# Earlier aggregation loads, other chunk counts in batch 0, and an x conversion moved ahead of a batch's last root

## The chip, the cores and the metric

The kernel runs on one core of a Trainium2 chip. The metric is the device time of one launch in microseconds; 1651.48 us is the median of three runs before the change.

## The reference

Eight batches of x (2048 rows of 512), one adjacency matrix (2048 x 2048, 0 or 1, about 0.8% ones), weights W (512 x 1024) and a bias.

```python
Wi, Wj = (W[:, :Din], W[:, Din:])
mi = jnp.einsum('bkd,od->bko', x, Wi)
mj = jnp.einsum('bkd,od->bko', x, Wj)
a = adj.astype(x.dtype)
deg = a.sum(axis=1)
out = deg[None, :, None] * (mi + b) + jnp.einsum('ij,bjo->bio', a, mj)
...
x = _layernorm(x + out, axis=-1)
```

## The kernel before

A batch is 16 tiles of 128 rows. Each batch has two phases. In the **projection** PE computes mj (half h = 0) and mi (h = 1) for each tile. fp32 products are made of fp32r matmuls: `parts` (ScalarE, lines 430 and 432) turns a tile of x into `x_hi` and `x_lo`, `difference` (POOL, line 268) makes `x_df`, and `project` (PE) runs 4 cross matmuls (line 330) and 8 main ones (lines 338 and 340) per half, 24 per tile. ScalarE copies the cross result out of PSUM (`take_cross`), VectorE combines (lines 559 and 566) and splits the next x (`split_x`, lines 548 and 551), ScalarE takes mj_hi (line 445) and POOL mj_lo (line 273). mi goes to DRAM (`store_mi`, line 179) and comes back later (`load_mi`, line 198). Tiles 0 and 1 of batch 0 are computed natively (`project_native`, line 315) from `x_first` and the weights as loaded (`w_stage`), while VectorE splits the weights (`split_w`, lines 527 to 533, last part `W_df`).

In the **aggregation** PE multiplies the adjacency matrix with mj, 32 matmuls (line 362) per tile into one of two PSUM buffers. ScalarE widens the adjacency columns of tile i+2 to fp32r when tile i is done (`widen`, line 457). POOL adds the bias to the reloaded mi (`add_bias`, line 279), VectorE forms `residual` (line 594: deg * mi + x in a ring of four buffers r) and then `normalise` (lines 600 to 619), for which ScalarE gives the square root (`root`, line 461). SyncE stores the tile (line 246). Aggregation tile i may start when VectorE has summed tile i-2 (line 600).

The adjacency matrix arrives during batch 0 as 64 chunks through four buffers (`load_chunk`, line 175): ScalarE casts each to int8 (`cast_chunk`, line 452), VectorE adds it into the degree sums (`count_chunk`, lines 577 and 580), and a chunk load waits for both of the chunk four before it. Every 16 chunks PE sums them over partitions (`degrees`, line 347) and VectorE takes the result (`take_degrees`, line 585). The lists say how many chunks are handled in each tile:

```python
PROJ_CHUNKS = [0, 0, 2, 2, 2, 2, 2, 2, 2, 2, 2, 2, 2, 2, 2, 2]
AGG_CHUNKS = [4, 3, 3, 3, 3, 4, 4, 4, 4, 4, 0, 0, 0, 0, 0, 0]
```

Each engine's order is written out by hand and the engines meet only at semaphores. SyncE issues all loads and stores but those of x_raw, which ScalarE issues. At the end of a batch's projection SyncE issues five loads for the aggregation (mi of tiles 0 and 1, x of tiles 0, 1, 2 into r). In VectorE's order residual(0) stands behind the projection, then for each tile come its counts, residual(i+1) and normalise(i). Batch 0 is unrolled; batches 1 to 6 are one hardware loop, batch 7 a copy, with inner hardware loops over groups of four tiles.

Of the kernel before, what the change touches and what calls it, by code (L numbers as in the profile page):

```python
# [5 lines left out]
def bass_adj_resnorm(nc, x, xt, adjt, wt, b, out):  # L6
# [33 lines left out]
    with ctx:  # L40
# [90 lines left out]
        norm_ready = sem("norm_ready")  # L131
        out_stored = [sem(f"out_stored{s}") for s in range(GT)]
# [5 lines left out]
        AGG_CHUNKS = [4, 3, 3, 3, 3, 4, 4, 4, 4, 4, 0, 0, 0, 0, 0, 0]  # L138
# [31 lines left out]
        def _(sp):  # L170
# [11 lines left out]
            for c in range(DK, 2 * DK):  # L182
                sp.dma_start(w_stage[c][:, :], wt[c]).then_inc(w_loaded[c], 16)
# [19 lines left out]
            def batch(bt):  # L203
                zero = known(bt) and bt == 0
                base = NT * bt

                def proj(g):
                    for u in range(GT):
                        if zero and GT * g + u < NATIVE:
                            continue  # L210
                        if zero:
                            for c in proj_chunks(GT * g + u):
                                load_chunk(c + AB)
                        store_mi(base + GT * g + u)

                over_groups(sp, zero, False, proj)

                sp.wait_ge(mi_stored, 16 * (base + 2))
                for u in range(2):
                    load_mi(base + u, u)  # L220
                for u in range(GT - 1):
                    if not zero:
                        sp.wait_ge(out_stored[u], 16 * NG * bt)
                    load_r(base + u, u)

                def agg(g):
                    for u in range(GT):
# [18 lines left out]
                        sp.dma_start(out_tiles[m], r[u][:, :]).then_inc(out_stored[u], 16)  # L246
# [59 lines left out]
        def _(pe):  # L306
# [60 lines left out]
            def batch(bt):  # L367
# [15 lines left out]
                if zero:  # L383
                    for i in range(NT):
                        if i == 2:
                            degrees(1)
# [22 lines left out]
        def _(act):  # L409
# [52 lines left out]

            for order in range(DK):
# [11 lines left out]
            def batch(bt):  # L475
# [3 lines left out]
                def proj(g):  # L479
                    last_group = known(g) and g == NG - 1  # L480
                    for u in range(GT):
# [4 lines left out]
                        if not (final and last_group and u == GT - 1):  # L486
# [14 lines left out]
                over_groups(act, zero, True, proj)  # L501
                if zero:
                    for i in range(NT):
                        for c in agg_chunks(i):
                            cast_chunk(c)
                        if i < NT - 2:
                            act.wait_ge(agg_done, i + 1)
                            widen(i + 2, i % 2, NT * ((i + 2) // TPB + 1))
                        root(i)
                else:  # L510
# [6 lines left out]
                    for i in range(2):  # L517
                        root(NT * bt + NT - 2 + i)

            over_batches(act, batch)  # L520

        @block.vector
        def _(dve):
# [73 lines left out]
            def normalise(m, u, s):  # L597
# [21 lines left out]
                nc.vector.tensor_scalar(r[u][:, :], r[u][:, :], mean_var[:, 0:1], inv_std[:, :],  # L619
                                        ALU.subtract, ALU.mult).then_inc(norm_ready, 1)  # L620
# [11 lines left out]
            def batch(bt):  # L632
# [25 lines left out]
                def agg(g):  # L658
                    for u in range(GT):
                        i = GT * g + u  # L660
                        m = base + i
                        if zero:
                            for c in agg_chunks(i):
                                count_chunk(c)
                            if i == 2:
# [8 lines left out]
                        normalise(m, u, u % 2)  # L674
# [41 lines left out]
```

## Time and profile before

| what | us |
|---|---|
| median of three runs | 1651.48 (1648.02 to 1652.07) |
| the profiled execution | 1650.52 |
| its span | 1648.7 |
| PE busy (matmul) | 1637.6 |
| VectorE busy | 848.3 |
| ScalarE busy | 662.3 |
| POOL busy | 499.8 |

The mean granted TensorE clock of the span is 0.998 of full speed. The span is from the first to the last instruction; the profiled execution's time holds 1.8 us beside it. Busy time says which engine is never long idle; the rest is read from the starts of PE's matmuls and from what ended each engine's idle time.

### The profile page before, as it was taken

The numbers are of one execution on the slowest core, as the hardware profiler recorded it, in microseconds if no ns is written. First come the engines' busy times: TensorE is split into PE (matmuls) and PEld (weight loads), VectorE is DVE, ScalarE is ACT, GpSimd is POOL, SyncE is SP. The second block draws the span as 40 slices with busy tenths as digits, with TensorE's granted clock in tenths as the row PEclk, the third lists the DMA queues.
The fourth block names the chain that finished last, engine by engine and source line by source line (L and its number), as shares of the span: only waits on it lengthen the run. The fifth ranks groups of instructions, "written<-read, shape, count | busy, mean of one in ns | idle before, by whom it ended". The sixth has DMA issues, their size and how long they took to land.

```text
span 1648.7 us, 24789 instructions
## 1 busy us (share of the span) xinstructions
PE 1637.6 (99%) x7196; PEld 1347.3 (82%) x7196; DVE 848.3 (51%) x1878; ACT 662.3 (40%) x964; POOL 499.8 (30%) x386
## 2 busy tenths in 40 slices
PE   9999999999999999999999999999999999999998
PEld 6878888888888888888888888888888888888886
DVE  8778644445445444445444445445444445444544
ACT  5755434423353324533245322453325522255221
POOL 3531134311343113431144311442114421154210
PEclk9999999999999999999999999999999999999999
DMA  6667423333223332343322432233323243232332
GB/s 198 196 197 240 147 77 102 128 108 96 89 90 127 115 95 83 99 131 102 95 95 89 134 109 87 90 102 126 109 83 101 90 138 104 76 102 83 128 115 70
DMA packets 102698, 187.26 MB, mean 114 GB/s; under 512 B 11408, under 2 KB 11408, under 8 KB 102672
## 3 DMA queue, kind: packets, MB, share of 16 engines
q1 hardware_dynamic: 84816, 154.44, 29.4%
q10 hardware_dynamic: 17856, 32.51, 6.4%
q8 instruction: 11, 0.18, 0.0%
q14 instruction: 15, 0.12, 0.0%
HBM read 119.80 MB, written 67.11 MB: 113 GB/s over the span
## 4 chain that ended last, share of the span: by engine, by line
PE 91%; issue 2%; DVE 1%; DMA 0%; POOL 0%; DVEq 0%; SPq 0%; ACT 0%; POOLq 0%
PE agg_ps L362 54%; PE cross_ps L330 12%; PE main_ps L340 12%; PE main_ps L338 12%; DMA mi_in<-mi_dram 0%; POOL mi_in L279 0%; DVE deg_part L580 0%; DVEq L601 0%; DVE r L600 0%; DVE stats L602 0%; POOL x_df L268 0%; DVE r L619 0%; PE deg_ps L347 0%; DVE newton L611 0%; SPq L246 0%
## 5 line engine op out<-in xcount | busy, mean ns | idle before, releaser
L362 PE MATMUL agg_ps<-mj_hi,adjT 128*128 128x512 f32 x2048 | 798.0, 390 | 1.7 <-DVE r L600 1.7
L362 PE MATMUL agg_ps<-mj_lo,adjT 128*128 128x512 f32 x2048 | 797.5, 389 | 0.0
L457 ACT ACTIVATE adjT<-adjT 128x2048 fp32r (+1 forms) x128 | 245.2, 1916 | 532.4 <-PE agg_ps L362 532.4
L362 PEld LDWEIGHTS agg_ps<-mj_hi,adjT 128*128 128x128 f32 x2048 | 385.0, 188 | 81.7 <-DVE r L600 1.8
L362 PEld LDWEIGHTS agg_ps<-mj_lo,adjT 128*128 128x128 f32 x2048 | 385.0, 188 | 80.0
L338 PE MATMUL main_ps<-W_hi,x_hi 128*128 128x512 f32 x1008 | 392.3, 389 | 0.0
L340 PE MATMUL main_ps<-W_lo,x_lo 128*128 128x512 f32 x1008 | 392.2, 389 | 0.0
L279 POOL TENSOR_TENSOR mi_in<-mi_in,bias 128x512 f32<-128x512 f32 x128 | 166.1, 1300 | 655.9 <-DMA mi_in<-mi_dram 655.8
L330 PE MATMUL cross_ps<-W_df,x_df 128*128 128x512 f32 x1008 | 270.8, 390 | 1.0 <-DVE W_df L533 0.5
L273 POOL TENSOR_TENSOR mj_lo<-mj,mj_hi 128x512 f32 (+1 forms) x126 | 169.7, 1347 | 269.7 <-ACT mj_hi L445 269.7
L600 DVE TENSOR_TENSOR r<-agg_ps,r 128x512 f32<-128x512 f32 x128 | 88.4, 691 | 315.7 <-PE agg_ps L362 315.7
L441 ACT ACTIVATE cross<-cross_ps 128x512 f32<-128x512 f32 x252 | 148.4, 589 | 209.7 <-PE cross_ps L330 208.2
L268 POOL TENSOR_TENSOR x_df<-x_top,x_lo 128x512 fp32r<-128x512 f32 x126 | 163.9, 1301 | 202.9 <-ACT x_lo L432 202.7
L330 PEld LDWEIGHTS cross_ps<-W_df,x_df 128*128 128x128 f32 x1008 | 188.4, 188 | 43.3 <-ACT cross L441 2.7
L338 PEld LDWEIGHTS main_ps<-W_hi,x_hi 128*128 128x128 f32 x1008 | 189.2, 188 | 39.7 <-DVE mi L566 0.2
L340 PEld LDWEIGHTS main_ps<-W_lo,x_lo 128*128 128x128 f32 x1008 | 189.2, 188 | 39.4
L559 DVE SCALAR_TENSOR_TENSOR mj<-main_ps,cross 128x512 f32<-128x512 f32 x126 | 87.0, 690 | 215.1 <-PE main_ps L340 208.4
L566 DVE SCALAR_TENSOR_TENSOR mi<-main_ps,cross 128x512 f32<-128x512 f32 x126 | 87.0, 691 | 115.9 <-PE main_ps L340 102.3
L594 DVE SCALAR_TENSOR_TENSOR r<-mi_in,deg,r 128x512 f32<-128x512 f32 x128 | 98.0, 768 | 53.6 <-DMA r<-in_x 42.3
L430 ACT ACTIVATE x_hi<-x_top 128x512 fp32r<-128x512 f32 x126 | 79.6, 632 | 66.1 <-PE main_ps L340 63.0
L602 DVE BATCH_NORM_STATS2 stats<-r 128x6 f32<-128x512 f32 x128 | 88.9, 695 | 11.7
L551 DVE TENSOR_TENSOR x_raw<-x_raw,x_top 128x512 f32<-128x512 f32 x126 | 87.2, 692 | 4.3
(59 smaller groups left out, 600.3 us busy)
## 6 DMA issues: line engine op xcount, KB each, us to landing
mi_dram<-mi SPq DMA_DIRECT2D x128, 256.0 KB, 2.1
mi_in<-mi_dram SPq DMA_DIRECT2D x128, 256.0 KB, 2.7
r<-in_x SPq DMA_DIRECT2D x128, 256.0 KB, 2.7
out<-r SPq DMA_DIRECT2D x128, 256.0 KB, 2.1
x_raw<-in_xt ACTq DMA_DIRECT2D x124, 256.0 KB, 2.8
adj_in<-in_adjt SPq DMA_DIRECT2D x64, 256.0 KB, 3.6
r<-in_wt SPq DMA_DIRECT2D x4, 256.0 KB, 5.4
adj_in<-in_xt SPq DMA_DIRECT2D x2, 256.0 KB, 3.8
```

The lines of the kernel that those rows point to most:

```text
L268: pool.tensor_tensor(x_df[s][:, :], x_top[:, :], x_lo[s][:, :].bitcast(fp32), ALU.subtract).then_inc(x_df_ready, 1)
L273: pool.tensor_tensor(mj_lo[:, bass.ds(t, 1), :].rearrange("p t d -> p (t d)"), mj[:, :], mj_hi[:, bass.ds(t, 1), :].rearrange("p t d -> p ...
L279: pool.tensor_tensor(mi_in[u % 2][:, :], mi_in[u % 2][:, :], bias[:, :], ALU.add).then_inc(mib_ready, 1)
L330: last = nc.tensor.matmul(cross_ps[h][:, :], x_df[s][:, k * P:(k + 1) * P], W_df[:, half * DK + k, :], start=(k == 0), stop=(k == DK - 1))
L338: nc.tensor.matmul(main_ps[h][:, :], x_hi[s][:, k * P:(k + 1) * P], W_hi[:, half * DK + k, :], start=(k == 0), stop=False)
L340: last = nc.tensor.matmul(main_ps[h][:, :], x_lo[s][:, k * P:(k + 1) * P], W_lo[:, half * DK + k, :], start=False, stop=(k == DK - 1))
L362: last = nc.tensor.matmul(agg_ps[s][:, :], adjT[s][:, j, :], part[:, j, :], start=(j == 0 and part is mj_hi), stop=(j == NT - 1 and part i ...
L441: nc.scalar.activation(cross[h][:, :], cross_ps[h][:, :], ACT.Copy).then_inc(cross_ready, 1)
L457: nc.scalar.activation(adjT[s][:, :, :], adjT8[:, :, bass.ds(i * P, P)], ACT.Copy).then_inc(adjT_ready, 1)
L594: nc.vector.scalar_tensor_tensor(r[u][:, :], mi_in[u % 2][:, :], deg[:, bass.ds(i, 1)], r[u][:, :], ALU.mult, ALU.add).then_inc(res_ready, 1)
L600: nc.vector.tensor_tensor(r[u][:, :], agg_ps[s][:, :], r[u][:, :], ALU.add).then_inc(sum_ready, 1)
L602: nc.vector.bn_stats(stats[:, :], r[u][:, :]).then_inc(ln_step, 1)
```

## The change

Five edits. (1) `first_loads` (the five loads) is issued by SyncE in the last projection group behind the store of its second tile (tile 13), in every batch; in batch 0 the store of mi also goes ahead of a tile's last chunk load. (2) In batch 0 the chunk counts per aggregation tile are other ones, and the degree step of chunks 16 to 31 stands ahead of tile 3 instead of 2. (3) ScalarE converts x of the next batch's tile 1 ahead of the root of a batch's last tile, and not in the next batch's first tile; its group loop is therefore split. (4) The first weight block is loaded from ScalarE's queue. (5) The last tile of the last batch is scaled in two halves of the columns, and the second half is stored by ScalarE.

```diff
@@ -129,13 +129,14 @@
         ln_step = sem("ln_step")
         std_ready = sem("std_ready")
         norm_ready = sem("norm_ready")
+        last_stored = sem("last_stored")
         out_stored = [sem(f"out_stored{s}") for s in range(GT)]
 
         block = ctx.enter_context(nc.Block())
 
         CHUNKS = IB * NT
         PROJ_CHUNKS = [0, 0, 2, 2, 2, 2, 2, 2, 2, 2, 2, 2, 2, 2, 2, 2]
-        AGG_CHUNKS = [4, 3, 3, 3, 3, 4, 4, 4, 4, 4, 0, 0, 0, 0, 0, 0]
+        AGG_CHUNKS = [2, 3, 3, 3, 3, 3, 3, 4, 4, 4, 4, 0, 0, 0, 0, 0]
 
         def proj_chunks(t):
             first = sum(PROJ_CHUNKS[:t])
@@ -179,7 +180,7 @@
                 sp.dma_start(mi_dram[n], mi[:, :]).then_inc(mi_stored, 16)
 
             sp.dma_start(x_first[0], xt[0]).then_inc(x_first_loaded[0], 16)
-            for c in range(DK, 2 * DK):
+            for c in range(DK + 1, 2 * DK):
                 sp.dma_start(w_stage[c][:, :], wt[c]).then_inc(w_loaded[c], 16)
             sp.dma_start(x_first[1], xt[1]).then_inc(x_first_loaded[1], 16)
             for c in range(DK):
@@ -202,26 +203,35 @@
 
             def batch(bt):
                 zero = known(bt) and bt == 0
+                final = known(bt) and bt == NB - 1
                 base = NT * bt
+
+                def first_loads():
+                    if zero:
+                        sp.wait_ge(w_ready, 2 * DK)
+                        sp.wait_ge(main_done, 2 * NATIVE)
+                    sp.wait_ge(mi_stored, 16 * (base + 2))
+                    for u in range(2):
+                        load_mi(base + u, u)
+                    for u in range(GT - 1):
+                        if not zero:
+                            sp.wait_ge(out_stored[u], 16 * NG * bt)
+                        load_r(base + u, u)
 
                 def proj(g):
                     for u in range(GT):
                         if zero and GT * g + u < NATIVE:
                             continue
                         if zero:
-                            for c in proj_chunks(GT * g + u):
+                            for c in proj_chunks(GT * g + u)[:-1]:
                                 load_chunk(c + AB)
                         store_mi(base + GT * g + u)
-
-                over_groups(sp, zero, False, proj)
-
-                sp.wait_ge(mi_stored, 16 * (base + 2))
-                for u in range(2):
-                    load_mi(base + u, u)
-                for u in range(GT - 1):
-                    if not zero:
-                        sp.wait_ge(out_stored[u], 16 * NG * bt)
-                    load_r(base + u, u)
+                        if zero:
+                            load_chunk(proj_chunks(GT * g + u)[-1] + AB)
+                        if known(g) and g == NG - 1 and u == 1:
+                            first_loads()
+
+                over_groups(sp, zero, True, proj)
 
                 def agg(g):
                     for u in range(GT):
@@ -243,7 +253,10 @@
                                 if c + AB < CHUNKS:
                                     load_chunk(c + AB)
                         sp.wait_ge(norm_ready, m + 1)
-                        sp.dma_start(out_tiles[m], r[u][:, :]).then_inc(out_stored[u], 16)
+                        if final and ending and u == GT - 1:
+                            sp.dma_start(out_tiles[m, :, 0:DO // 2], r[u][:, 0:DO // 2]).then_inc(out_stored[u], 16)
+                        else:
+                            sp.dma_start(out_tiles[m], r[u][:, :]).then_inc(out_stored[u], 16)
 
                 agg(0)
                 if zero:
@@ -382,7 +395,7 @@
 
                 if zero:
                     for i in range(NT):
-                        if i == 2:
+                        if i == 3:
                             degrees(1)
                         if i == 7:
                             degrees(2)
@@ -460,6 +473,7 @@
                 act.wait_ge(ln_step, LN * m + 3)
                 nc.scalar.activation(std[:, :], var_eps[:, :], ACT.Sqrt).then_inc(std_ready, 1)
 
+            act.dma_start(w_stage[DK][:, :], wt[DK]).then_inc(w_loaded[DK], 16)
             for order in range(DK):
                 copy_w_hi(DK + order, order)
             native_mj_hi(0)
@@ -483,7 +497,7 @@
                         n = NT * bt + t
                         if zero and t < NATIVE:
                             continue
-                        if not (final and last_group and u == GT - 1):
+                        if not (final and last_group and u == GT - 1) and (zero or not (known(g) and t == 0)):
                             parts(n + 1, (u + 1) % 2)
                         take_cross(n, 0)
                         if not (final and last_group and u >= GT - 3):
@@ -498,7 +512,14 @@
                         if last_group and u in (0, 2):
                             widen(u // 2, u // 2, NT if zero else None)
 
-                over_groups(act, zero, True, proj)
+                if zero:
+                    for g in range(NG):
+                        proj(g)
+                else:
+                    proj(0)
+                    with act.Fori(1, NG - 1) as g:
+                        proj(g)
+                    proj(NG - 1)
                 if zero:
                     for i in range(NT):
                         for c in agg_chunks(i):
@@ -506,6 +527,8 @@
                         if i < NT - 2:
                             act.wait_ge(agg_done, i + 1)
                             widen(i + 2, i % 2, NT * ((i + 2) // TPB + 1))
+                        if i == NT - 1:
+                            parts(NT + 1, 1)
                         root(i)
                 else:
                     with act.Fori(0, NP - 1) as k:
@@ -515,9 +538,14 @@
                             widen(2 * k + i + 2, i, None)
                             root(m)
                     for i in range(2):
+                        if i == 1 and not final:
+                            parts(NT * bt + NT + 1, 1)
                         root(NT * bt + NT - 2 + i)
 
             over_batches(act, batch)
+            act.wait_ge(norm_ready, TILES + 1)
+            act.dma_start(out_tiles[TILES - 1, :, DO // 2:DO], r[GT - 1][:, DO // 2:DO]).then_inc(last_stored, 16)
+            act.wait_ge(last_stored, 16)
 
         @block.vector
         def _(dve):
@@ -594,7 +622,7 @@
                 nc.vector.scalar_tensor_tensor(r[u][:, :], mi_in[u % 2][:, :], deg[:, bass.ds(i, 1)], r[u][:, :],
                                                ALU.mult, ALU.add).then_inc(res_ready, 1)
 
-            def normalise(m, u, s):
+            def normalise(m, u, s, last_tile):
                 dve.wait_ge(res_ready, m + 1)
                 dve.wait_ge(agg_done, m + 1)
                 nc.vector.tensor_tensor(r[u][:, :], agg_ps[s][:, :], r[u][:, :], ALU.add).then_inc(sum_ready, 1)
@@ -616,8 +644,9 @@
                 dve.wait_ge(ln_step, LN * m + 6)
                 nc.vector.tensor_tensor(inv_std[:, :], inv0[:, :], newton[:, 1:2], ALU.mult).then_inc(ln_step, 1)
                 dve.wait_ge(ln_step, LN * m + 7)
-                nc.vector.tensor_scalar(r[u][:, :], r[u][:, :], mean_var[:, 0:1], inv_std[:, :],
-                                        ALU.subtract, ALU.mult).then_inc(norm_ready, 1)
+                for cols in ((slice(0, DO // 2), slice(DO // 2, DO)) if last_tile else (slice(0, DO),)):
+                    nc.vector.tensor_scalar(r[u][:, cols], r[u][:, cols], mean_var[:, 0:1], inv_std[:, :],
+                                            ALU.subtract, ALU.mult).then_inc(norm_ready, 1)
 
             for order in range(DK):
                 split_w(DK + order, order)
@@ -662,7 +691,7 @@
                         if zero:
                             for c in agg_chunks(i):
                                 count_chunk(c)
-                            if i == 2:
+                            if i == 3:
                                 take_degrees(1)
                             if i == 7:
                                 take_degrees(2)
@@ -671,7 +700,7 @@
                         ending = known(g) and g == NG - 1 and u == GT - 1
                         if not ending:
                             residual(m + 1, i + 1, (u + 1) % GT, 16 * (NG * bt + g + 1 + (u + 1) // GT))
-                        normalise(m, u, u % 2)
+                        normalise(m, u, u % 2, final and ending)
 
                 if zero:
                     for g in range(NG):
```

## Rows read from the trace of the kernel before

**Rows 1.** The page, busy time: engine, us, share, instructions.

```profile
PE 1637.6 (99%) x7196; PEld 1347.3 (82%) x7196; DVE 848.3 (51%) x1878; ACT 662.3 (40%) x964; POOL 499.8 (30%) x386
```

**Rows 2.** Timeline of PE, 110 to 118: start, us, engine, line, operation, idle before.

```profile
110.87 0.39 PE L362 MATMUL agg_ps<-mj_lo,adjT 128*128 128x512 f32 x1
112.19 0.61 PE L347 MATMUL deg_ps<-ones,deg_part 128*128 128x2 f32 x4 [0.94 <-DVE deg_part L580]
114.47 0.79 PE L362 MATMUL agg_ps<-mj_hi,adjT 128*128 128x512 f32 x1 [1.67 <-DVE r L600]
115.06 0.63 PE L362 MATMUL agg_ps<-mj_lo,adjT 128*128 128x512 f32 x1
...
117.92 0.40 PE L362 MATMUL agg_ps<-mj_hi,adjT 128*128 128x512 f32 x1
```

**Rows 3.** Timeline of PE around a later degree step.

```profile
152.38 0.50 PE L347 MATMUL deg_ps<-ones,deg_part 128*128 128x2 f32 x4
...
153.07 0.40 PE L362 MATMUL agg_ps<-mj_lo,adjT 128*128 128x512 f32 x1
```

**Rows 4.** Timeline of the other engines, 89 to 109.

```profile
89.69 0.42 SPq L179 DMA_DIRECT2D mi_dram<-mi  x1
...
92.75 2.05 SPq L175 DMA_DIRECT2D adj_in<-in_adjt  x2
...
96.17 1.82 POOL L273 TENSOR_TENSOR mj_lo<-mj,mj_hi 128x512 fp32r<-128x512 f32 x1 [0.62 <-ACT mj_hi L445]
...
101.40 0.96 SPq L198 DMA_DIRECT2D mi_in<-mi_dram  x2
...
105.93 2.67 POOL L279 TENSOR_TENSOR mi_in<-mi_in,bias 128x512 f32<-128x512 f32 x2 [7.94 <-DMA mi_in<-mi_dram]
105.97 1.28 ACT L461 ACT_TABLE_LOAD   x1
107.98 1.17 DVE L594 SCALAR_TENSOR_TENSOR r<-mi_in,deg,r 128x512 f32<-128x512 f32 x1 [7.51 <-POOL mi_in L279]
```

**Rows 5.** Timeline of PE and POOL at two passages between batches.

```profile
426.28 1.29 POOL L268 TENSOR_TENSOR x_df<-x_top,x_lo 128x512 fp32r<-128x512 f32 x1 [17.70 <-ACT x_lo L432]
...
427.02 0.39 PE L340 MATMUL main_ps<-W_lo,x_lo 128*128 128x512 f32 x1
427.70 0.72 PE L330 MATMUL cross_ps<-W_df,x_df 128*128 128x512 f32 x2 [0.30 <-POOL x_df L268]
...
429.97 1.29 POOL L268 TENSOR_TENSOR x_df<-x_top,x_lo 128x512 fp32r<-128x512 f32 x1
...
630.71 0.39 PE L340 MATMUL main_ps<-W_lo,x_lo 128*128 128x512 f32 x1
631.14 0.72 PE L330 MATMUL cross_ps<-W_df,x_df 128*128 128x512 f32 x2
```

**Rows 6.** Timeline of VectorE in later aggregation tiles of batch 0, and in the last tile.

```profile
158.39 2.28 DVE L580 TENSOR_TENSOR deg_part<-deg_part,adj_in 128x512 fp32r<-128x512 f32 x3 [0.54 <-DMA adj_in<-in_adjt]
...
168.71 0.68 DVE L600 TENSOR_TENSOR r<-agg_ps,r 128x512 f32<-128x512 f32 x1
...
172.21 3.07 DVE L580 TENSOR_TENSOR deg_part<-deg_part,adj_in 128x512 fp32r<-128x512 f32 x4
...
1642.60 0.69 DVE L600 TENSOR_TENSOR r<-agg_ps,r 128x512 f32<-128x512 f32 x1 [3.66 <-PE agg_ps L362]
```

**Rows 7.** Timeline of the start: SyncE, VectorE, PE.

```profile
1.19 0.90 SPq L183 DMA_DIRECT2D mi_in<-in_wt  x2
...
4.33 0.43 DVE L527 TENSOR_SCALAR adjT<-mi_in 128x512 uint32<-128x512 uint32 x1 [4.33 <-DMA mi_in<-in_wt]
...
22.00 1.20 PE L330 MATMUL cross_ps<-W_df,x_df 128*128 128x512 f32 x4 [0.47 <-DVE W_df L533]
```

**Rows 8.** Timeline of the end.

```profile
1645.64 0.55 DVE L619 TENSOR_SCALAR r<-r,mean_var,inv_std 128x512 f32<-128x512 f32 x1
1646.22 0.33 SPq L246 DMA_DIRECT2D out<-r  x1
```

## The prediction

> **What bounds the kernel now.** I read the page first: PE is busy for 1637.6 of 1648.7 us [rows 1]. So no engine's speed is at issue; only the stretches in which PE's matmuls do not follow each other at their full beat can be won. I then went along PE's timeline and took the distances between the starts of matmuls. A matmul normally starts 0.227 us after the one before it (1637.6 us over 7196 matmuls gives 0.228; 32 of them make an aggregation tile, 7.26 us; 24 make a projection tile, 5.44 us). Four kinds of places break the beat.
>
> First, one stall in batch 0 ahead of aggregation tile 2 [rows 2]. After the matmul at 110.87 the small degree matmuls come at 112.19, tile 2 starts only at 114.47, and then matmuls start 0.43 us apart (115.06 - 114.47 is even 0.59): the clock has gone to 1.2 GHz, its lower level, after PE had run two matmul groups with waits of 1 to 2 us. By 117.92 the beat is full again (2.4 GHz). Second, five of the seven passages from one batch to the next lose a little at the start of projection tile 1 [rows 5]. Third, PE waits at 22.00 for the weights' third part [rows 7]. Fourth, after the last matmul some 6 us of normalising and storing follow, in which PE does nothing [rows 8].
>
> **Part 1, the stall in batch 0.** From 110.87 to 117.92 are 7.05 us. The work in it is nine full-beat matmuls, 9 x 0.227 = 2.04 us, and the degree step. What a degree step costs where nobody waits is seen ahead of tile 7 [rows 3]: 153.07 - 152.38 = 0.69, less one beat = 0.46 us. So 7.05 - 2.04 - 0.46 = 4.55 us are lost, the slow clock included.
>
> The cause, followed back [rows 4]: PE's tile 2 needs VectorE's sum of tile 0 (line 600), which is queued behind residual(0), four counts and residual(1). residual(0) started only at 107.98, after 7.51 us of waiting for POOL's bias, which waited 7.94 us for the load of mi that SyncE issued at 101.40, behind all projection stores and chunk loads. The degree matmuls moreover waited for chunk 31, the fourth of those counts.
>
> The change puts the five loads behind the store of tile 13, which was issued at 89.69 to 90.11. Five issues take what they took before, 0.96 us for the two of mi (101.40) and about 1.45 for the three of r, so they end near 92.55; SyncE had its next issue at 92.75 anyway, waiting for a count. The queue's order costs nothing there. The two stores that now follow five transfers could land later: the mi load needed 4.5 us from issue (101.40) to POOL's start at 105.93 in traffic, so I put the last of five at 97 to 98, and the store of tile 14 at about 98 to 100. VectorE's copy of tile 15 waits for that store; nobody on PE waits for this copy until the next batch. POOL becomes free at 96.17 + 1.82 = 97.99 and adds the bias by 99.3 and 100.6. VectorE then does residual(0) around 100.5 to 102.5, two counts instead of four (2 x 0.77, as four take 3.07 at 172.21 [rows 6]), residual(1) 0.75, so it is ready for the sum of tile 0 between 103 and 106, while PE ends tile 0 only at 103.85. The sum ends by 107 at the latest, and PE asks for it at 111.1: cover of at least 4 us. One thing becomes late next, without reaching PE: the square root's table load (1.28 us at 105.97) now stands in tile 0's normalisation and delays it about 1 us; tile 1's sum then comes near 112.0 and is asked for at 118.8. I take the full 4.55 us. Bounds: 4.6 above; below, 1.6 if the stall shrinks only until the clock holds (the eight matmuls from 114.47 to 117.92 took 3.45 instead of 1.81).
>
> **The moved counts.** Chunks per tile go from 4,3,3,3,3,4,4,4,4,4 to 2,3,3,3,3,3,3,4,4,4,4. The total is 36 both times, so no work is saved; what moves is who has slack. The degree step of tile 3 needs chunk 31, counted in tile 1: a tile of slack. That of tile 7 needs chunk 47, now counted during tile 6, and that of tile 11 needs chunk 63, now counted during tile 10; both had a whole tile of slack before. Working for the latter [rows 6]: the sum starts at 168.71 and the four counts of the next tile end at 172.21 + 3.07 = 175.28, 6.57 us later. A sum that waits for PE starts about 0.26 us after the end of its tile (1642.60, where the last matmul starts at 1642.11 and is due for 0.23), so the last count ends 6.83 us into a tile of 7.26: 0.43 us of slack. For tile 7, with three counts, it is 1.2 us. VectorE also waited 0.54 us for a chunk at 158.39. One such wait exceeds the slack of tile 11 by 0.1. I take 0, and 0 to 0.8 us of loss as range.
>
> **Part 2, the batch passages.** The last matmul of tile 0 starts at 427.02, tile 1 at 427.70 [rows 5]: 0.45 us over the beat, and 0.15 more until the beat is regained, 0.60 together. At 630.71 to 631.14 it is 0.20 + 0.13 = 0.33; three further passages (834, 1038, 1241) show the same 0.33. Passages 218.8 and 1444 show 0.03. Tile 1 waited for x_df, which POOL computed at 426.28 after ScalarE's two conversions, which stand behind the square root of the last tile. The change issues both conversions ahead of that root. Their inputs were split at the end of the projection, so they run while ScalarE would wait for tile 15; 1.2 us of ScalarE and 1.3 of POOL hidden under a 7.26 us tile. What is late next is the copy of cross 0, which used to come after the two conversions and comes 1.1 us earlier without them, well ahead of PE. Gain: 0.60 + 4 x 0.33 less 5 x 0.03 = 1.8 us (bounds 1.2 and 1.9).
>
> **Part 3, the start.** SyncE issues x first and the first weight at 1.19; VectorE starts on it at 4.33 and its chain of splits ends in the wait at 22.00 [rows 7]. ScalarE can issue that load beside SyncE's, 0.44 us earlier. The transfers share their engines, so I take 0.3 us for VectorE's chain. PE's own first matmul is bound by the 28 warm-up matmuls, but at 22.00 (idle 0.47, 0.64 off the beat) and at the tile after it PE waits on VectorE's chain, more than 0.3 in sum, so the 0.3 arrives. Bounds: 0 and 0.44. If ScalarE's table load (1.28 long) came ahead of the issue, the weight would be 0.85 late instead.
>
> **Part 4, the end.** The last scaling takes 0.55 us at 1645.64, the store is issued at 1646.22 [rows 8]. In two halves the first store goes out about 0.2 us sooner, the second about 0.1 later from another queue, each with half the bytes. I take 0.25 us, bounds -0.3 and +0.5 (no half-size store is in the trace).
>
> **Other edits.** The store ahead of the second chunk load, and the unrolled loops of SyncE and ScalarE, cost nothing where those engines wait for others. In ScalarE's new loop the parts of tile 2 follow a loop entry; x_df of tile 2 ended at 429.97 + 1.29 = 431.26 and PE asked for it at about 433.3, 2.0 us of cover.
>
> **Sum**: 4.55 + 1.8 + 0.3 + 0.25 = 6.9 us. The profiled execution took 1650.52 us (span 1648.7), the median of three is 1651.48, 0.96 above it. Against its own time the sum gives 1643.6; the comparison is with the median, so I forecast 1651.48 - 6.9 = 1644.6 us.
>
> **Rivals.** (A) Tile 11's degree step waits for chunk 63. For it: 0.43 us of slack against a wait of 0.54 seen once. Against it: the other chunk groups came in time. PE loses 0.3 to 0.8 us, the clock should hold as it did over the 0.45 us gap at 427: about 1645.1, chance 0.14. (B) The two loads or stores on a second queue bring nothing, because the transfers fill the same DMA engines: start and end give 0, 6.35 us remain, 1645.1, chance 0.12. The Trainium skill, "DMA: Bandwidth & Descriptors", section "Issuing engines are not separate DMA queues", says that issuing from several engines saves only the sequencer's issue time; that is this rival, and by it the start could give at most the 0.44 of one issue. (C) The first weight comes late, behind the table load or on a slow first use of the queue: 0.85 us later, and the clock's rise after the warm-up may suffer, 1 to 2 us lost in place of 0.3 won: 1646.4, chance 0.05. (D) The stall stays because something else holds residual(0), such as the crowd of transfers around 90 to 100: then only parts 2 to 4 count, 1649.1, chance 0.07. (E) Slower: entering ScalarE's new loop stops its sequencer (fetching the code) in each of seven batches. It decides from 2.0 us of entry on, the cover of x_df for tile 2; to eat 6.9 us it must be 3.0 us, and 3.7 us for a loss of 0.3%, 1656.4. Nothing near that is in the trace. Chance 0.03.
>
> **Chances.** The forecast has 0.59. A measurement can tell about 0.3% (4.95 us), a time below 1646.5. Forecast, A and B lie below it, but runs of the kernel before scatter by 4 us, so a part of them falls short: faster 0.77, same 0.20 (D, half of C, scatter), slower 0.03. Range: best bounds sum to 7.5 us, with about 2 us for scatter 1642.0; at the top A and C with scatter, 1648.2; D and E stay outside, about 0.1.
>
> **What would show it.** Right: PE's starts stay 0.227 apart through 111 to 118 with the clock at full; residual(0) near 101; tile 1 of each batch on the beat and POOL's x_df for it inside the last aggregation tile; a first split near 4.0. Wrong: a PE wait for deg_part (A), a first split later than 4.33 (C), VectorE waiting for mi_in past 104 (D), PE waiting for x_df of tile 2 (E).

## The result and the profile after

The changed kernel takes 1643.48 us (median of six runs, 1643.4 to 1643.72). Beside it the kernel before took 1651.86 us (1648.02 to 1652.68). The ratio is 0.9952 with a 95% interval of 0.9941 to 0.9962: faster by 0.5%, inside the forecast range, 1.1 us below the forecast 1644.6. The profiled execution took 1643.72 us with a span of 1641.9 (before: 1650.52 and 1648.7).

The changed kernel's page, busy time by engine and the chain of work that ended last by engine:

```profile
PE 1634.2 (100%) x7196; PEld 1346.8 (82%) x7196; DVE 844.8 (51%) x1879; ACT 661.7 (40%) x964; POOL 498.4 (30%) x386
...
PE 98%; DVE 1%; DMA 0%; issue 0%; POOL 0%; ACT 0%; DVEq 0%
```

PE is 3.4 us less busy with the same 7196 matmuls [rows 1]. In the 7.05 us of the old stall it counted as busy for 4.44, where the same matmuls at full beat take 2.5: at the low clock a matmul counts as longer. Most of the rest lies at the passages, where the profile's modelled end of a matmul (0.39 us after its start) covers most of PE's delay. Next, all waits of PE in the changed kernel (engine, line, releaser: us, times, longest):

```profile
PE agg_ps L415 <- POOL ones L277: 1.1, 1, 1.1
PE cross_ps L343 <- DVE W_df L561: 0.5, 1, 0.5
```

The waits for VectorE's sum and for the degree count [rows 2] are gone. Both that remain are in the first 22 us. Around the place of the old stall the timelines of SyncE, POOL, VectorE and ScalarE read (start, us, engine, line, operation, idle before):

```profile
88.00 0.34 SPq L180 DMA_DIRECT2D mi_dram<-mi  x1
...
89.59 0.92 SPq L199 DMA_DIRECT2D mi_in<-mi_dram  x2
...
90.56 1.38 SPq L202 DMA_DIRECT2D r<-in_x  x3
...
92.58 0.33 SPq L176 DMA_DIRECT2D adj_in<-in_adjt  x1
...
97.66 2.99 POOL L292 TENSOR_TENSOR mi_in<-mi_in,bias 128x512 f32<-128x512 f32 x2
...
101.12 0.74 DVE L622 SCALAR_TENSOR_TENSOR r<-mi_in,deg,r 128x512 f32<-128x512 f32 x1
...
101.79 1.48 DVE L608 TENSOR_TENSOR deg_part<-deg_part,adj_in 128x512 fp32r<-128x512 f32 x2
...
103.18 0.75 DVE L622 SCALAR_TENSOR_TENSOR r<-mi_in,deg,r 128x512 f32<-128x512 f32 x1
...
103.98 0.69 DVE L628 TENSOR_TENSOR r<-agg_ps,r 128x512 f32<-128x512 f32 x1
...
105.84 1.28 ACT L474 ACT_TABLE_LOAD   x1
```

Against [rows 4]: SyncE issues the loads at 89.59 instead of 101.40, POOL adds the bias at 97.66 instead of 105.93, residual(0) starts at 101.12 instead of 107.98, and tile 0's sum at 103.98, as soon as PE has finished that tile. PE asks for it at 111.0, so some 6 us of cover stand here. The five issues fit ahead of SyncE's next one at 92.58.

PE itself runs through, and the granted clock stays up. PE's timeline from tile 1 to tile 2:

```profile
110.74 0.39 PE L375 MATMUL agg_ps<-mj_lo,adjT 128*128 128x512 f32 x1
110.96 0.39 PE L375 MATMUL agg_ps<-mj_hi,adjT 128*128 128x512 f32 x1
111.19 0.39 PE L375 MATMUL agg_ps<-mj_lo,adjT 128*128 128x512 f32 x1
```

The stretch of the old stall in the changed kernel (window, its length, busy times of PE, PEld, VectorE, ScalarE and POOL, then granted clock, DMA share, GB/s):

```profile
110.87:117.92 7.05, 7.05 (x33) 5.84 (x32) 5.90 (x14) 3.90 (x5) 1.30 (x1) 1.00 0.75 253
```

At the first passage inside the batch loop, POOL's x_df for tile 1 now lies in the last aggregation tile, 9 us before PE needs it, and PE keeps its beat (422.34 to 422.56), against 0.68 us at 427.02 [rows 5]:

```profile
413.44 1.44 POOL L281 TENSOR_TENSOR x_df<-x_top,x_lo 128x512 fp32r<-128x512 f32 x1 [9.66 <-ACT x_lo L445]
...
422.34 0.39 PE L353 MATMUL main_ps<-W_lo,x_lo 128*128 128x512 f32 x1
422.56 0.62 PE L343 MATMUL cross_ps<-W_df,x_df 128*128 128x512 f32 x2
```

**Where the time went, by the two traces.** The matmuls are the same in number and order, so the start of one and the same matmul can be compared. Just ahead of the old stall it is 110.87 before and 110.74 after: 0.13 us won at the start, less than the scatter there (see the experiments). The first matmul of aggregation tile 7 of batch 0 starts at 152.74 and 148.10: 4.64, so 4.51 at the stall. The last matmul starts at 1642.11 and 1635.45: 6.65 (from unrounded starts), so 2.0 at the passages. From the last matmul to the end of the span it is 6.59 and 6.45: 0.14 at the end. In sum 6.8 us. The medians differ by more, 8.4, and the kernel before scatters by over 4 us where the new one stays within 0.3. Half of the study is about that difference.

### The profile page after: what moved, and what is told of

Read it like the earlier page. It is cut to its first block, busy times and chain, and to the rows that moved or that the text cites. A ratio compares the mean times of both kernels' runs of the same rounds, so it can differ in the third digit from the quotient of the medians.

```text
span 1641.9 us, 24654 instructions
## 1 busy us (share of the span) xinstructions
PE 1634.2 (100%) x7196; PEld 1346.8 (82%) x7196; DVE 844.8 (51%) x1879; ACT 661.7 (40%) x964; POOL 498.4 (30%) x386
## 4 chain that ended last, share of the span: by engine, by line
PE 98%; DVE 1%; DMA 0%; issue 0%; POOL 0%; ACT 0%; DVEq 0%
PE agg_ps L375 57%; PE cross_ps L343 14%; PE main_ps L351 14%; PE main_ps L353 14%; DVE W_lo L558 0%; DVE W_df L561 0%; DMA mi_in<-in_wt 0%; DVE adjT L555 0%; DVE x_raw L579 0%; DVE mj_lo L568 0%; PE deg_ps L360 0%; POOL x_df L281 0%; DVE x_top L576 0%; DVE stats L630 0%; DVE r L628 0%
## 5 line engine op out<-in xcount | busy, mean ns | idle before, releaser
L622 DVE SCALAR_TENSOR_TENSOR r<-mi_in,deg,r 128x512 f32<-128x512 f32 x128 | 101.4, 796 | 13.1 <-POOL mi_in L292 9.2
```

Source lines behind the costliest of these rows:

```text
L622: nc.vector.scalar_tensor_tensor(r[u][:, :], mi_in[u % 2][:, :], deg[:, bass.ds(i, 1)], r[u][:, :], ALU.mult, ALU.add).then_inc(res_ready, 1)
```

## The experiments

Each kernel below is an edit of the changed kernel, except one. Beside each group of them the kernel before ran along; its medians were 1649.4, 1650.4 and 1651.1 us. With the six runs beside the result that makes 65 runs from 1647.71 to 1654.84, median 1650.72, so the change is worth 7.1 us against all of them and the 8.4 holds part of this scatter. The new kernel's median hardly moves, so I compare with it.

**The base again.** No edit.

> The changed kernel once more, as the base for the others: 1643.5 us, its runs within 0.3 us of each other. If the small scatter of its first six runs was luck, it spreads over 2 to 4 us like the kernel before.

Measured: 1643.65 us, 1643.59 to 1643.80 over five runs; ratio to before 0.9965 [0.9951, 0.9978]. The kernel before, in eleven runs beside it: 1647.89 to 1651.36. The small scatter belongs to the new kernel.

**One edit taken back at a time, small ones.**

```diff
u1_weight_on_sync
-            for c in range(DK + 1, 2 * DK):
+            for c in range(DK, 2 * DK):
...
-            act.dma_start(w_stage[DK][:, :], wt[DK]).then_inc(w_loaded[DK], 16)
```

> The changed kernel with the first weight block loaded from SyncE's queue again. My theory: the gain of this edit is bounded by the shared transfer engines, and the traces of before and after differ by 0.13 us at this place, so 1643.6, 0.1 to 0.2 above the base, first split of VectorE at 4.3. The rival, that the issue time of 0.44 us arrives in full as I forecast in part: 1643.8 or more.

Measured: 1643.70 us (1643.62 to 1644.08), 0.05 above the base. The first split of the changed kernel starts at 4.15 instead of 4.33, although the load is issued 0.44 earlier:

```profile
0.75 0.42 ACTq L476 DMA_DIRECT2D mi_in<-in_wt  x1
0.75 0.39 SPq L182 DMA_DIRECT2D adj_in<-in_xt  x1
...
4.15 0.43 DVE L555 TENSOR_SCALAR adjT<-mi_in 128x512 uint32<-128x512 uint32 x1 [4.15 <-DMA mi_in<-in_wt]
```

Against the kernel before 0.18 of 0.44 us reached VectorE; against u1's own trace, where the first split starts at 4.25, it is 0.10. The median shows 0.05. What reached PE stays open: the last matmul ahead of the old stall starts at 110.87, 111.05 and 111.12 in the three traces with the load on SyncE's queue behind x (the kernel before, u1, w2 below), and anywhere from 110.49 to 111.73 in those with it on ScalarE's.

```diff
u2_whole_last_store
-                        if final and ending and u == GT - 1:
-                            sp.dma_start(out_tiles[m, :, 0:DO // 2], r[u][:, 0:DO // 2]).then_inc(out_stored[u], 16)
-                        else:
-                            sp.dma_start(out_tiles[m], r[u][:, :]).then_inc(out_stored[u], 16)
+                        sp.dma_start(out_tiles[m], r[u][:, :]).then_inc(out_stored[u], 16)
...
-                        normalise(m, u, u % 2, final and ending)
+                        normalise(m, u, u % 2, False)
```

> The changed kernel with the last tile scaled and stored whole. By the traces of before and after the end shrank by 0.15 us, so 1643.65. Rival: the halves gain nothing and the 0.15 was scatter of one transfer, 1643.5.

Measured: 1643.87 us (1643.61 to 1643.88), 0.22 above the base. With one run at the base's level this is small but goes the expected way. The traces are clearer: from the last matmul to the end it is 6.59 to 6.60 us in the three with a whole last store, and 6.45 to 6.49 in all others.

**The passages.**

```diff
u3_conversion_late
-                        if not (final and last_group and u == GT - 1) and (zero or not (known(g) and t == 0)):
+                        if not (final and last_group and u == GT - 1):
                             parts(n + 1, (u + 1) % 2)
...
-                        if i == NT - 1:
-                            parts(NT + 1, 1)
...
-                        if i == 1 and not final:
-                            parts(NT * bt + NT + 1, 1)
```

> The changed kernel with the x conversion of a batch's tile 1 back behind the last root. My theory: five passages lose 0.33 to 0.60 again, 2.0 us in sum, 1645.5, and PE waits for x_df at the start of tile 1 there. Rival: the passages' loss came from ScalarE's loop entries and not from the conversion; then it stays at 1643.5, since the loop stays split here.

Measured: 1644.60 us (1644.28 to 1644.85), 0.95 above the base. Both expectations missed: a late conversion costs half of what the traces had shown. What was left in u3 was ScalarE's split loop, so the next kernel put the one loop back too.

```diff
w1_conversion_late_one_loop (beside the edit of u3)
-                if zero:
-                    for g in range(NG):
-                        proj(g)
-                else:
-                    proj(0)
-                    with act.Fori(1, NG - 1) as g:
-                        proj(g)
-                    proj(NG - 1)
+                over_groups(act, zero, True, proj)
```

> As u3_conversion_late, and ScalarE's groups again in one loop as in the kernel before. u3 cost 1.0 us and not the 2.0 that the traces of before and after differ by. Theory: the other 1.0 is the loop entry that stood ahead of the conversion at each passage and is gone with the unrolled first group; then this kernel is at 1645.6 and its five passages lose 0.60 and 4 x 0.33 in the trace. Rival: the rest was scatter or came from elsewhere (the early loads), 1644.6.

Measured: 1645.96 us (1645.66 to 1646.49), 2.3 above the base. The two traces side by side, u3 first: ScalarE's root and conversion at the first looped passage and PE at the next one.

```profile
419.79 0.20 ACT L474 ACTIVATE std<-var_eps 128x1 f32<-128x1 f32 x1 [7.35 <-DVE var_eps L630]
420.31 0.63 ACT L443 ACTIVATE x_hi<-x_top 128x512 fp32r<-128x512 f32 x1 [0.32 <-PE main_ps L353]
...
625.99 0.39 PE L353 MATMUL main_ps<-W_lo,x_lo 128*128 128x512 f32 x1
626.22 0.73 PE L343 MATMUL cross_ps<-W_df,x_df 128*128 128x512 f32 x2
```

```profile
419.64 0.20 ACT L474 ACTIVATE std<-var_eps 128x1 f32<-128x1 f32 x1 [7.34 <-DVE var_eps L623]
420.37 0.63 ACT L443 ACTIVATE x_hi<-x_top 128x512 fp32r<-128x512 f32 x1 [0.52 <-PE main_ps L353]
...
626.04 0.39 PE L353 MATMUL main_ps<-W_lo,x_lo 128*128 128x512 f32 x1
626.47 0.49 PE L343 MATMUL cross_ps<-W_df,x_df 128*128 128x512 f32 x1
```

From the root to the conversion ScalarE takes 0.52 us without a loop entry between them and 0.73 with one. These 0.2 us arrive in full at PE: from the last matmul of tile 0 to the first of tile 1 it is 0.23 us in u3 and 0.43 in w1, the old gap. From the last matmul of batch 0 to the last of all PE takes 1421.65 us in the changed kernel, 1422.62 in u3, 1423.64 in w1 and 1423.66 in the kernel before. So with the conversion late, root and conversion cost 0.97 us and the loop entry another 1.02, five times 0.2. A kernel with the conversion early and one loop was not run: the early conversion may take away both, since the entry then stands behind it.

**The stall: which part carries it.**

```diff
u4_loads_late
-                        if known(g) and g == NG - 1 and u == 1:
-                            first_loads()

                 over_groups(sp, zero, True, proj)
+                first_loads()
```

> The changed kernel with the five loads issued behind the whole projection again; the new chunk counts stay. Theory 1 (the stall was one queue on VectorE, and either part removes most of it): residual(0) near 108, then two counts, residual(1), and the sum of tile 0 ends near 112.1 instead of 114.4; PE waits 0.4 to 1.9 us ahead of tile 2, too short for the clock to fall: 1644.0 to 1645.4, runs close together. Theory 2 (the early loads carry the whole gain, the counts nothing): PE waits as before and the clock falls, about 1648.

Measured: 1644.59 us (eight runs 1644.02 to 1645.16, one 1648.22), 0.9 above the base. Theory 1 holds in size, but not in detail. The one run at 1648.22 has a mean granted clock of 0.998 where the others have 0.999 or more, so "too short for the clock to fall" does not hold for all. And in its trace, of the fastest run, PE's tile 2 is late by a tenth of a microsecond only, because stores ahead of chunk loads let the five loads out at 99.71 rather than 101.40, and VectorE has two counts less. So the changed store order has a share in u4's small loss, and where the median's 0.9 us lie this trace does not show:

```profile
106.33 1.75 DVE L621 SCALAR_TENSOR_TENSOR r<-mi_in,deg,r 128x512 f32<-128x512 f32 x1 [7.13 <-POOL mi_in L291]
...
110.49 0.39 PE L374 MATMUL agg_ps<-mj_lo,adjT 128*128 128x512 f32 x1
110.80 0.50 PE L374 MATMUL agg_ps<-mj_hi,adjT 128*128 128x512 f32 x1
```

```diff
u5_old_counts
-        AGG_CHUNKS = [2, 3, 3, 3, 3, 3, 3, 4, 4, 4, 4, 0, 0, 0, 0, 0]
+        AGG_CHUNKS = [4, 3, 3, 3, 3, 4, 4, 4, 4, 4, 0, 0, 0, 0, 0, 0]
...
-                        if i == 3:
+                        if i == 2:
                             degrees(1)
...
-                            if i == 3:
+                            if i == 2:
                                 take_degrees(1)
```

> The changed kernel with the chunk counts 4,3,3,3,3,4,4,4,4,4 and the degree step ahead of tile 2 again; the loads stay early. Theory 1: residual(0) at 101, four counts end by about 105.5 and the sum by 107, before PE asks at 111: no wait, 1643.5. Theory 3 (the loads alone are not enough, since four counts and the degree step hold tile 2): PE waits 1 us or more, 1644.5 to 1648.

Measured: 1643.60 us (1643.40 to 1643.64), the base's time. With early loads the counts change nothing, as theory 1 has it.

u6_both_back has the edits of u4 and u5 together.

> The changed kernel with both parts of the stall back (late loads, old counts); start, passages and end stay as changed. Theory 1: the stall is whole again, +4.5 us or more by the trace. Theory 4 (the scatter of the kernel before, 1648.0 to 1652.7, comes from how long the clock stays at its low level behind this stall): the runs spread over 2 us or more, between about 1646 and 1650. If the scatter had another source they stay within 0.5 us of each other near 1648.

Measured: 1647.23 us, 3.6 above the base, eleven runs from 1644.75 to 1649.43. The slowest is the profiled one; its trace loses 5.3 us at the stall. Neither part alone is missed by more than 0.9, both together cost 3.6: they remove the same wait, and their gains do not add. The scatter is back with the stall. The three stretches behind the stall in u6's profiled execution (window, its length, busy times, granted clock, DMA share, GB/s), and below them two of the kernel before:

```profile
114.14:117.50 3.36, 3.36 (x8) 2.68 (x9) 2.69 (x10) 2.13 (x5) 0.00 (x0) 0.50 0.28 104
117.50:120.50 3.00, 3.00 (x8) 2.32 (x8) 2.81 (x5) 1.43 (x1) 0.25 (x1) 0.53 0.61 195
120.60:123.00 2.40, 2.40 (x12) 1.99 (x11) 1.86 (x9) 1.26 (x3) 0.93 (x1) 1.00 0.95 299
```

```profile
114.47:117.80 3.33, 3.33 (x8) 2.65 (x9) 2.65 (x10) 2.10 (x5) 0.00 (x0) 0.51 0.27 100
117.90:121.00 3.10, 3.10 (x15) 2.56 (x14) 2.90 (x5) 1.37 (x1) 0.09 (x1) 1.00 0.63 201
```

PE stayed at 1.2 GHz for over 6 us in u6 and for 3.4 in the kernel before, although the break ahead of it was the shorter one in u6: 3.0 us from the last matmul of tile 1 to the first of tile 2, against 3.6. At that level a matmul starts 0.427 us after the last, 0.2 later than at 2.4 GHz, so u6's stretch costs about 3 us and the other 1.6.

**The gap by itself.** The changed kernel with one wait of PE ahead of tile 2, for a later (v2) or much later (v3) step of tile 1's normalisation.

```diff
+                        if i == 2:
+                            pe.wait_ge(ln_step, LN + 3)      (v2_forced_wait)
+                            pe.wait_ge(norm_ready, 2)        (v3_forced_wait_long)
                         aggregate(0, i, i % 2, i == 0, i >= 2)
```

> The changed kernel with one wait added: PE's aggregation tile 2 of batch 0 waits for the variance of tile 1 (ready near 113.2), so PE idles once for 2.1 us at the place of the old stall and nothing else is late. If only the idle time costs: 1645.8 with runs within 0.4. Theory 4 (the clock falls after such a gap in some runs and for unequal times): 1646 to 1649, spread over 1 us or more, matmuls 0.43 us apart behind the gap.

> As v2_forced_wait, but tile 2 waits for tile 1's scaled result (near 114.9): one idle gap of 3.8 us. If only the idle time costs: 1647.5. Theory 4: the clock falls in nearly every run, so 1.5 to 3.5 us more, 1649 to 1651.

Measured: v2 has two groups. Five runs took 1646.02 to 1646.60 with a mean granted clock of 0.999, six took 1647.77 to 1648.84 with 0.998. Its profiled execution (1646.18) is of the first kind, PE idle for 2.10 us and on the beat at once. The first group is the base plus the gap, 1643.65 + 2.26 = 1645.9; the second adds 1.7 to 2.8 us. That the clock fell in the second group is read from its mean and the time; none of the six was profiled. v3 took 1648.81 to 1650.86 in eleven runs (median 1649.58), none near 1647.5: the gap's 3.9 us and 2 us on top, of which the eight matmuls at the low clock in its trace explain 1.6. (The profiled execution, 1650.40, also came to tile 1's end 1.0 us late, from the start and from a wait shown below.) In v3's trace the clock falls only after PE has resumed:

```profile
115.87 0.50 PE L375 MATMUL agg_ps<-mj_hi,adjT 128*128 128x512 f32 x1 [3.76 <-DVE r L650]
...
116.91 0.51 PE L375 MATMUL agg_ps<-mj_hi,adjT 128*128 128x512 f32 x1
117.22 0.63 PE L375 MATMUL agg_ps<-mj_lo,adjT 128*128 128x512 f32 x1
117.64 0.63 PE L375 MATMUL agg_ps<-mj_hi,adjT 128*128 128x512 f32 x1
```

**The early loads on the kernel before.** Only the five loads move; counts, store order, conversion, start and end are those of before.

```diff
w2_before_early_loads (against the kernel before)
+                def first_loads():
...
                         store_mi(base + GT * g + u)
+                        if known(g) and g == NG - 1 and u == 1:
+                            first_loads()

-                over_groups(sp, zero, False, proj)
-
-                sp.wait_ge(mi_stored, 16 * (base + 2))
-                for u in range(2):
-                    load_mi(base + u, u)
...
+                over_groups(sp, zero, True, proj)
```

> The kernel before with one thing changed: the five loads go out behind the store of tile 13. Theory 1: the stall is gone by this alone, no PE wait between 108 and 118, about 1643.5 + 2.0 (passages) + 0.2 (start and end) = 1645.7. Theory 4 (the scatter belongs to the stall): the runs lie within 0.5 us of each other. If the scatter belongs to something else of the kernel before (the batch passages, the start), they spread over 2 us or more, as before's own do.

Measured: 1647.05 us, 4.0 below the kernel before beside it (1651.09; ratio 0.9976 [0.9967, 0.9985]), so this one move carries about half of the change. But the runs spread from 1646.23 to 1649.73 and the median is 1.3 above what I expected: theory 4 is not the whole story. There is no stall at 111 in its trace. There is one at 61, in the projection, where ScalarE and PE wait for VectorE:

```profile
61.01 0.69 DVE L572 SCALAR_TENSOR_TENSOR mi<-main_ps,cross 128x512 f32<-128x512 f32 x1 [1.75 <-DMA mi_dram<-mi]
...
61.79 0.60 ACT L447 ACTIVATE cross<-cross_ps 128x512 f32<-128x512 f32 x1 [1.48 <-DVE mi L572]
...
61.75 0.19 PEld L344 LDWEIGHTS main_ps<-W_hi,x_hi 128*128 128x128 f32 x1 [0.55 <-DVE mi L572]
61.75 0.50 PE L344 MATMUL main_ps<-W_hi,x_hi 128*128 128x512 f32 x1
```

VectorE may not write mi again before the last mi is stored. The store sat behind chunk loads in SyncE's queue until 56.32, 1.0 us after mi was ready, and landed 4.7 us later; PE waited for VectorE and lost 0.3 us. The waits of that kind in all of a trace, the kernel before first, then w2, then the changed kernel:

```profile
DVE mi L566 <- DMA mi_dram<-mi: 13.2, 12, 2.5
```

```profile
DVE mi L572 <- DMA mi_dram<-mi: 10.8, 11, 2.0
```

```profile
DVE mi L594 <- DMA mi_dram<-mi: 1.8, 2, 1.0
```

In the twelve traces with the store ahead of a tile's last chunk load it occurs one to three times, 0.5 to 2.6 us in sum. But the chain to PE is no mark of the old order: it is there in u1, u6 and v3 too, near 34, and costs most in v3, 0.6 us:

```profile
34.40 0.69 DVE L596 SCALAR_TENSOR_TENSOR mi<-main_ps,cross 128x512 f32<-128x512 f32 x1 [1.32 <-DMA mi_dram<-mi]
...
35.15 0.50 PE L351 MATMUL main_ps<-W_hi,x_hi 128*128 128x512 f32 x1 [0.44 <-DVE mi L596]
```

The store it waits for was issued at 28.65 and not held up in the queue; it was slow to land. Some 0.8 us of w2's median are left over (1647.05 less 1643.65 + 2.3 for the passages and less 0.25 for start and end), and most of its scatter. w2 differs otherwise only in the counts, which u5 showed to be worth nothing with the new store order. That points to the store order, but it is not shown: the one chain seen in w2 costs 0.3 us, and a kernel with the store order alone taken back was not run.

**A try at something faster.**

```diff
v1_weight_first
+            sp.dma_start(w_stage[DK][:, :], wt[DK]).then_inc(w_loaded[DK], 16)
             sp.dma_start(x_first[0], xt[0]).then_inc(x_first_loaded[0], 16)
...
-            act.dma_start(w_stage[DK][:, :], wt[DK]).then_inc(w_loaded[DK], 16)
```

> The changed kernel with SyncE issuing the first weight block ahead of the first x tile. Theory: the transfers are the limit, the one issued first lands near 3.6 us, so VectorE's chain starts 0.5 earlier and PE's first matmul 0.1 to 0.3 later (x lands near 4.3); PE's waits at 21.8 and 24.9 for that chain shrink by more than that, 1643.1. Rival: PE's later first matmul shifts all behind it and the waits do not shrink, 1643.7.

Measured: 1643.64 us (1643.44 to 1644.08), the base's time. In its trace the gap ahead of the cross matmuls near 21 shrinks, 0.37 from start to start against 0.87, but PE arrives there later by 0.23, and the last matmul starts at 1635.32 against 1635.45. The traces of u4 and v2, whose start is that of the changed kernel, have 0.31 and 0.38 there, so one trace does not show the shorter gap as v1's doing. The chain of splits itself starts earlier, at 3.29 instead of 4.15, and no time comes of it. No kernel of this study is measurably faster than the changed one.

## Why the prediction was right, and where it was not

**The stall: right in cause and place, and in size for the profiled execution.** 4.55 us forecast, 4.51 in the traces. Both figures rest on the same execution of the kernel before, so they say that its stall went whole, not what it costs as a rule. The order of events came as worked out: five issues between the store of tile 13 and the next chunk load, POOL free at 97.7, residual(0) at 101.1 (forecast 100.5 to 102.5), table load inside tile 0's normalisation, tile 1's sum at 111.2 (forecast 112.0). What the working took from one execution was the length of the low clock. The stall costs 3.6 us in the median of u6, with runs from 1.1 to 5.8 above the base, and v2 shows why: the same gap has two prices. The sum was made against a profiled execution and set off from the median, and the scatter of the median was only put in the range. From the profiled execution it gave 1643.6, and the changed kernel's took 1643.72: that close a match is in part luck, since the terms of the stall, the start and the end were 0.04, 0.17 and 0.11 us too large and the passages 0.2 too small. The 8.4 of the medians is against six runs; against all 65 of the kernel before it is 7.1, and 6.2 of that are accounted for by u6, w1, u1 and u2 together. The other 0.9 us stay open.

**The counts: right.** Forecast as moving slack only; u5 shows zero. The slack of 0.43 us at tile 11's degree step was right too. The last two counts in the changed kernel's trace, and PE's degree step:

```profile
175.37 1.49 DVE L608 TENSOR_TENSOR deg_part<-deg_part,adj_in 128x512 fp32r<-128x512 f32 x2
...
177.26 0.50 PE L360 MATMUL deg_ps<-ones,deg_part 128*128 128x2 f32 x4
```

They end at 176.86, 0.40 before PE. Rival A did not occur there; in u4, where VectorE runs behind, the degree step ahead of tile 7 starts 0.26 us late (147.97 after a last matmul at 147.48). The slack is real and small.

**The passages: right in size, with a link of the chain unseen.** Forecast 1.8, traces 2.0, medians 2.3 (w1). The prediction saw the conversion behind the square root. It did not see that a loop entry stood between them, five times 0.2 us, and priced the split loop at nothing. Splitting the loop without moving the conversion saves half of the loss (w1 against u3). In the changed kernel this makes no difference that a run shows: the conversion stands ahead of the root and the entry, x_df is there 9 us early, and the whole 2.0 us is gone. How much of it the early conversion would have taken with one loop stays open.

**The start: too large, if it is there at all.** 0.3 forecast, 0.13 between the two traces, 0.05 in u1's median, and a scatter between executions that is larger. The 0.44 of issue time shrank to 0.18 or 0.10 at the landing. The first x tile is transferred at the same time: in v1, where the weight block is issued at the same 0.75 but x only behind it, VectorE's first split starts 0.86 us earlier, at 3.29. The prediction also held PE's first matmul to be bound by the warm-up; in the trace of before it waits 0.17 us for this very load:

```profile
4.45 2.28 PE L315 MATMUL main_ps<-mi_in,adj_in 128*128 128x512 f32 x4 [0.17 <-DMA mi_in<-in_wt]
```

Rival B was nearer here. The rule of the Trainium skill ("DMA: Bandwidth & Descriptors", "Issuing engines are not separate DMA queues"), that issuing from more engines saves only issue time, held as an upper bound: less than the issue time was saved.

**The end: right, somewhat too large.** 0.25 forecast, 0.14 in the traces, 0.22 in u2's median. Rival B, nothing from a second queue, does not hold here.

**The store order: priced at nothing, and open.** The rows that bear on it are the kernel before's waits of VectorE's mi copy for its own store, 13.2 us in twelve waits. PE lost less than 0.1 us behind them in the profiled execution, and I took one trace for cover. With the new order they shrink to one to three waits, and w2 leaves 0.8 us that may be theirs; no run shows that they are.

## What to carry to other kernels

When two edits shorten the same queue ahead of one wait, take their gain once: here each alone leaves at most 0.9 of 3.6 us. Gaps on TensorE like the 2.1 and 3.8 us here are priced by their idle time and, in part of the runs, by a stretch at half clock behind them, so a kernel with such a gap scatters. A kernel's scatter is a hint that one may be there, though w2 scattered by 3.5 us without one in its trace. Before pricing an edit of order or of a loop at nothing, look whether its engine stands in the chain that releases the bottleneck: here a loop entry of 0.2 us did.

## What the runs showed of the hardware

The clock need not fall in the gap: in v3 PE idled for 3.8 us at a granted clock of 1.00, resumed at full beat for five matmuls, and fell to 1.2 GHz some 1.2 us after resuming. After a gap of 2.1 us six of eleven runs show the time and the mean granted clock of a fall. The low stretch was 3.4 us in two profiles (the kernel before, v3) and over 6 in a third (u6). Only two beats of the fp32r matmuls with 512 columns were seen over any length, 0.227 and 0.427 us; the Trainium skill ("TensorE: Matmul & The Clock Gate", "What's actually happening") says the same, that the clock has two states and that idleness brings the lower one. A beat of 0.43 us alone does not tell the clock: the native fp32 matmuls of the start have it at a granted clock of 1.00. Entering a hardware loop cost ScalarE 0.2 us. A 256 KB store of mi that lands in 2.1 us in the median took over 5 in v3 near 30.
